# Attention on one Trainium2 core: the six working PSUM banks shared out anew between row maxima and scores

## The reference, cut to what matters

```python
# B, T, C = 8, 1024, 256; 16 heads of 16; fp32
x = x + 0.5 * ffn(layernorm(x))          # 8 experts, top 1, capacity 1024
x = x + attention(layernorm(x))
x = x + 0.5 * ffn(layernorm(x))

def attention(x):
    q, k, v = rope(x @ Wq.T + bq), rope(x @ Wk.T + bk), x @ Wv.T + bv
    att = (q @ k.T) / 4                  # per batch and head, 1024 x 1024
    att = where(causal, att, -1e10)
    att = softmax(att)                   # the row maximum is taken off first
    return (att @ v) @ Wp.T + bp
```

## Time and profile before

| | before |
|---|---|
| runs | 2608.2, 2610.9, 2621.66 us; median 2610.9 us |
| the profiled execution | 2593.98 us |
| span of its trace | 2592.2 us |
| mean granted TensorE clock | 0.913 |
| TensorE matmuls busy | 2175.9 us (84% of the span) |
| VectorE busy | 1695.1 us (65%) |
| ScalarE busy | 1280.3 us (49%) |
| GpSimd busy | 908.2 us (35%) |

### The profile page before, as it was taken

How to read it: one execution, slowest core, us unless ns; L and a number is a source line. 1 busy time by engine, 2 the same in 40 slices (tenths; PEclk the granted TensorE clock), 3 DMA queues, 4 the chain that set the end, 5 groups by cost and what they waited for, 6 DMA issues and landing times. The chain is left out here.

```text
span 2592.2 us, 42982 instructions
## 1 busy us (share of the span) xinstructions
PE 2175.9 (84%) x14628; PEld 1405.6 (54%) x14628; DVE 1695.1 (65%) x5128; ACT 1280.3 (49%) x2578; POOL 908.2 (35%) x1236
## 2 busy tenths in 40 slices
PE   4279999944799998999999999998994774899997
PEld 2169999933344344444434444443333764799997
DVE  7345655435778888788887878777854662565562
ACT  5334444411266656566566656666771333344443
POOL 3624444234233333333333333331001364344442
PEclk8689999967699999999999999999996775999999
DMA  9563222022544353444435344354405424423220
GB/s 367 191 204 115 74 96 99 26 68 87 135 102 106 97 120 95 109 101 107 110 95 119 88 103 101 87 120 94 87 26 165 138 83 164 139 74 103 81 74 22
DMA packets 187419, 283.24 MB, mean 109 GB/s; under 512 B 14888, under 2 KB 150248, under 8 KB 179008
## 3 DMA queue, kind: packets, MB, share of 16 engines
q1 hardware_dynamic: 172864, 247.12, 35.0%
q0 software_dynamic: 14336, 33.38, 3.7%
HBM read 154.02 MB, written 126.88 MB: 108 GB/s over the span
## 5 line engine op out<-in xcount | busy, mean ns | idle before, releaser
L1770 ACT ACTIVATE at_probs<-at_score_ps 128x512 f32<-128x512 f32 (+3 forms) x1536 | 692.2, 497 | 452.9 <-PE at_score_ps L1890 313.4
L1639 DVE CUSTOM_DVE_ANT_0 at_junk<-at_max_ps,at_causal 128x128 f32<-128x128 f32 (+3 forms) x1024 | 485.6, 484 | 127.4 <-PE at_max_ps L1876 125.3
L1876 PE MATMUL at_max_ps<-at_k,at_q 96*128 96x512 bf16 (+3 forms) x1536 | 493.9, 340 | 51.0 <-DVE at_peak L1639 31.2
L1887 PE MATMUL at_score_ps<-at_q,at_k 99*128 99x512 bf16 (+3 forms) x1536 | 499.1, 332 | 13.2 <-DMA at_v<-v_rows 5.4
L1642 DVE TENSOR_REDUCE at_peak<-at_max_ps 128x1 f32<-128x512 f32 x512 | 351.8, 687 | 115.3 <-PE at_max_ps L1876 112.0
L1876 PEld LDWEIGHTS at_max_ps<-at_k,at_q 96*128 96x128 bf16 x1536 | 144.5, 98 | 405.4 <-DVE at_peak L1639 192.4
L1089 DVE TENSOR_TENSOR f_hid_lo<-f_hid,f_hid_hi 128x512 fp32r<-128x512 f32 x256 | 177.5, 693 | 285.4 <-ACT f_hid_hi L1113 285.4
L1110 ACT ACTIVATE f_hid<-f_hid_ps 128x512 f32<-128x512 f32 x256 | 153.1, 598 | 377.9 <-PE f_hid_ps L1136 377.9
L1900 PE MATMUL at_o_ps<-at_probs,at_v 128*32 128x512 f32 (+3 forms) x3072 | 336.2, 510 | 1.3 <-ACT at_probs L1770 0.7
L1151 PE MATMUL f_y_ps<-f_w_hi,f_hid_hi 128*128 128x256 f32 x1024 | 290.9, 284 | 18.5 <-DVE f_hid_lo L1089 18.5
L1151 PE MATMUL f_y_ps<-f_w_hi,f_hid_lo 128*128 128x256 f32 x1024 | 291.2, 284 | 0.0
(11 more groups left out here) (222 smaller groups left out, 3547.4 us busy)
## 6 DMA issues: line engine op xcount, KB each, us to landing
f_w_raw<-in_w SPq DMA_DIRECT2D x32, 1024.0 KB, 7.6
qk<-at_parts SPq DMA_DIRECT2D x32, 768.0 KB, 4.2
expert_in<-r_zeros SPq DMA_DIRECT2D x16, 1040.0 KB, 12.7
f_xe<-expert_in SPq DMA_DIRECT2D x32, 520.0 KB, 6.6
v_rows<-at_v_outs SPq DMA_DIRECT2D x32, 512.0 KB, 6.2
at_v<-v_rows SPq DMA_DIRECT2D x32, 512.0 KB, 10.4
o_rows<-at_o_out SPq DMA_DIRECT2D x64, 256.0 KB, 2.0
at_q<-qk SPq DMA_DIRECT2D x32, 384.0 KB, 7.8
```

Source lines behind the costliest of these rows:

```text
L1639: v.tensor_tensor_reduce(junk[bank(k, r)][:, 0:w], src, causal[:, HALF - w:HALF], 1.0, LEAST, ALU.add, ALU.max, out).then_inc(max_used, 1)
L1770: a.activation(probs[t % 2][:, h, c0:c0 + w], score_ps[(GH * t + h) % BANKS][:, 0:w], ACT.Exp, scale=float(SCALE)).then_inc(exp_done, 1)
L1876: te.matmul(max_ps[bank(u, r)][:, 0:w], q[u][0:ROWS, h, i * P:(i + 1) * P], kk[u][0:ROWS, h, k0:k0 + w], start=True, stop=True).then_inc(m ...
L1887: last = te.matmul(out[:, 0:w], kk[u][:, h, j * P:(j + 1) * P], q[u][:, h, hf * HALF + c0:hf * HALF + c0 + w], start=True, stop=not diagonal)
```

## The change

Two bank counts take the place of one: two banks for scores, four for maxima. The semaphores' starting values and thresholds follow. The masked maxima write their masked values back over their own source in PSUM, and the `junk` tiles are gone. Of the early preparation, the v product goes to the output's bank and the two rotated tiles to the two score banks. The function `bank` takes the group in place of the slot, since the number of places is not a multiple of four.

```diff
--- before.py
+++ after.py
@@ -47,7 +47,7 @@
 ROWS_M = ROWS + PARTS
 VW = 2 * D
 SLOTS = 3
-BANKS = 3
+SCORE_BANKS, MAX_BANKS = 2, 4
 STEPS = [(0, j) for j in (0, 3, 2, 1)] + [(1, j) for j in (0, 7, 6, 5, 4, 1, 2, 3)]
 NS = len(STEPS)
 HALF = S // 2
@@ -1206,7 +1206,6 @@
         causal = sb("causal", [P, HALF], F32)
         hide = sb("hide", [P, P], F32)
         hide_bf = sb("hide_bf", [P, P], BF16)
-        junk = [sb(f"junk{k}", [P, HALF], F32) for k in range(BANKS)]
         stats = sb("stats", [P, 2, 6], F32)
         moments = sb("moments", [P, 2, 2], F32)
         half = sb("half", [P, 2], F32)
@@ -1239,8 +1238,8 @@
         o_out = [sb(f"o_out{k}", [P, HALF], F32) for k in range(2)]
         sums = sb("sums", [P, H * S // P], F32)
 
-        score_ps = [ps(f"score_ps{k}", [P, HALF]) for k in range(BANKS)]
-        max_ps = [ps(f"max_ps{k}", [P, HALF]) for k in range(BANKS)]
+        score_ps = [ps(f"score_ps{k}", [P, HALF]) for k in range(SCORE_BANKS)]
+        max_ps = [ps(f"max_ps{k}", [P, HALF]) for k in range(MAX_BANKS)]
         o_ps = ps("o_ps", [P, HALF])
         prep_ps = ps("prep_ps", [P, 2 * C])
 
@@ -1323,14 +1322,14 @@
 
             return NR * g + (0 if isinstance(g, int) and g == GROUPS else r)
 
-        def bank(k, r):
-
-            return place(k, r) % BANKS
-
-        EARLY_XT, EARLY_QK, EARLY_V, EARLY_ROT = max_ps[0], max_ps[1:3], score_ps[0], score_ps[1:3]
-
-        def peaks_in_ps(k, r):
-            return max_ps[bank(k, r)][:].bitcast(BF16)[0:PARTS * GH, 0:HALF]
+        def bank(g, r):
+
+            return place(g, r) % MAX_BANKS
+
+        EARLY_XT, EARLY_QK, EARLY_V, EARLY_ROT = max_ps[0], max_ps[1:3], o_ps, score_ps
+
+        def peaks_in_ps(g, r):
+            return max_ps[bank(g, r)][:].bitcast(BF16)[0:PARTS * GH, 0:HALF]
 
         @block.sync
         def _(sp):
@@ -1473,7 +1472,7 @@
             def move_peaks(g, u, half):
 
                 at = place(g, RING.index(FIRST)) if half == 0 else place(g + 1, RING.index(SECOND))
-                wait_apart(pool, max_used, at + BANKS + 1, sh.passed)
+                wait_apart(pool, max_used, at + MAX_BANKS + 1, sh.passed)
                 p.dma_start(q[u][ROWS:ROWS_M, :, half * HALF:(half + 1) * HALF], peak_t[:]
                             ).then_inc(peak_loaded[half], 16)
 
@@ -1627,16 +1626,16 @@
                     whose = g if half == 0 else g - 1
                     wait_apart(dve, max_ready, place(g, r) + 1, sh.passed)
                     dve.wait_ge(peak_loaded[1 - half], 16 * (whose + half))
-                    v.tensor_copy(peak_t[:], peaks_in_ps(k, r)).then_inc(max_used, 1)
+                    v.tensor_copy(peak_t[:], peaks_in_ps(g, r)).then_inc(max_used, 1)
                     return
                 half, n = RING[r]
                 h, i, k0, w, diagonal = ITEMS[half][n]
                 i -= half * TPB // 2
                 wait_apart(dve, max_ready, place(g, r) + 1, sh.passed)
                 out = (peak2 if k0 else peak[half])[:, i, h:h + 1]
-                src = max_ps[bank(k, r)][:, 0:w]
+                src = max_ps[bank(g, r)][:, 0:w]
                 if diagonal:
-                    v.tensor_tensor_reduce(junk[bank(k, r)][:, 0:w], src, causal[:, HALF - w:HALF], 1.0, LEAST,
+                    v.tensor_tensor_reduce(src, src, causal[:, HALF - w:HALF], 1.0, LEAST,
                                            ALU.add, ALU.max, out).then_inc(max_used, 1)
                 else:
                     v.tensor_reduce(out, src, AX.X, ALU.max).then_inc(max_used, 1)
@@ -1645,7 +1644,7 @@
 
                 at = (3 + 4) * g + 3 * half
                 if stage == 0:
-                    dve.wait_ge(max_used, (place(g, RING.index((1, 0))) if half == 0 else place(g + 1, 0)) + BANKS)
+                    dve.wait_ge(max_used, (place(g, RING.index((1, 0))) if half == 0 else place(g + 1, 0)) + MAX_BANKS)
                 else:
                     dve.wait_ge(peak_step, at + stage)
                 if half == 1:
@@ -1663,7 +1662,7 @@
                     v.tensor_tensor(peak_part[:, :, 2, :], peak_rest[:], peak_part[:, :, 1, :], ALU.subtract
                                     ).then_inc(peak_ready, 1)
 
-            dve.sem_inc(max_used, BANKS)
+            dve.sem_inc(max_used, MAX_BANKS)
             v.memset(kk[0][ROWS:ROWS_M], 1.0)
             measure(0)
             dve.wait_ge(w_hi_ready, 1)
@@ -1767,10 +1766,10 @@
                 act.wait_ge(pv_done, NS * g + t + 1)
                 for h in range(GH):
                     act.wait_ge(score_ready, GH * (NS * g + t) + h + 1)
-                    a.activation(probs[t % 2][:, h, c0:c0 + w], score_ps[(GH * t + h) % BANKS][:, 0:w],
+                    a.activation(probs[t % 2][:, h, c0:c0 + w], score_ps[(GH * t + h) % SCORE_BANKS][:, 0:w],
                                  ACT.Exp, scale=float(SCALE)).then_inc(exp_done, 1)
 
-            act.sem_inc(exp_done, BANKS)
+            act.sem_inc(exp_done, SCORE_BANKS)
             act.sem_inc(o_copied, 1)
             act.wait_ge(w_loaded, 16 * 3)
             a.copy(w_hi[:], w_raw).then_inc(w_hi_ready, 1)
@@ -1866,14 +1865,14 @@
                     pe.wait_ge(peak_ready, 2 * g + 1 if RING[r] == FIRST else 2 * g)
                     wait_apart(pe, max_used, place(g, r) + 1, sh.passed)
                     for i in range(TPB // 2):
-                        last = te.transpose(peaks_in_ps(u, r)[:, i * P:(i + 1) * P],
+                        last = te.transpose(peaks_in_ps(g, r)[:, i * P:(i + 1) * P],
                                             peak_part[:, i].rearrange("p a h -> p (a h)"), sh.ident_bf[:])
                     last.then_inc(max_ready, 1)
                     return
                 half, n = RING[r]
                 h, i, k0, w, _ = ITEMS[half][n]
                 pe.wait_ge(max_used, place(g, r) + 1)
-                te.matmul(max_ps[bank(u, r)][:, 0:w], q[u][0:ROWS, h, i * P:(i + 1) * P], kk[u][0:ROWS, h, k0:k0 + w],
+                te.matmul(max_ps[bank(g, r)][:, 0:w], q[u][0:ROWS, h, i * P:(i + 1) * P], kk[u][0:ROWS, h, k0:k0 + w],
                           start=True, stop=True).then_inc(max_ready, 1)
 
             def scores(g, u, t, h):
@@ -1883,7 +1882,7 @@
                 if t in FIRST_STEP.values() and h == 0:
                     pe.wait_ge(peak_loaded[hf], 16 * (g + 1))
                 pe.wait_ge(exp_done, GH * (NS * g + t) + h + 1)
-                out = score_ps[(GH * t + h) % BANKS]
+                out = score_ps[(GH * t + h) % SCORE_BANKS]
                 last = te.matmul(out[:, 0:w], kk[u][:, h, j * P:(j + 1) * P],
                                  q[u][:, h, hf * HALF + c0:hf * HALF + c0 + w], start=True, stop=not diagonal)
                 if diagonal:
@@ -1893,7 +1892,7 @@
             def times_v(g, u, t):
                 c0, w, _ = columns(STEPS[t])
                 hf, j = STEPS[t]
-                pe.wait_ge(exp_done, GH * (NS * g + t + 1) + BANKS)
+                pe.wait_ge(exp_done, GH * (NS * g + t + 1) + SCORE_BANKS)
                 if t == FIRST_STEP[hf]:
                     pe.wait_ge(o_copied, 2 * g + hf + 1)
                 for h in range(GH):
```

## The result

The changed kernel takes 2663.9 us (median of 4 runs, 2659.4 to 2665.9), the kernel before 2614.2 in the same comparison (4 runs, 2608.2 to 2621.7): a ratio of 1.0186 with a 95% interval of [1.0154, 1.0219], 49.7 us more. The forecast was 2653 in a range from 2613 to 2689, and slower. The size and the sign hold. Of the terms of its sum, three are right to a few hundredths of a microsecond, three are not.

A forecast was written before the change was run, and what follows sets the result against it. Waits between engines bound the loop, with VectorE the bound first and TensorE later in each prepared group. 26 groups at +1.18 us (+31), the last six +7 and the clock +4 gave +42 on 2610.9: 2653 us, range 2613 to 2689.

The forecast's parts named there:

- The walk through the VectorE stretch: First part of a prepared group, VectorE nearly full: with two score banks, waits for exponentials make TensorE 1.06 us later.
- The TensorE stretch: Later part of a prepared group, TensorE nearly full: score waits add 0.28 us in step 10 and 0.06 in step 8.
- The gain at the start of the next ring: At a group's end, before the next step 0 scores: four maxima banks let head 2 start 0.22 us earlier.
- The last six groups: The six groups behind the 26 with preparation: each was given the same 1.2 us loss, +7 us.
- The clock: Whole loop: more TensorE idling may bring clock falls (+22 us) or the new rhythm avoid them (-22); +4 taken.
- The write into PSUM: Masked maxima writing into PSUM instead of SBUF: bounded at -13 to +13 ns an operation, 0 us taken.
- A: ScalarE's exponentials come earlier, as TensorE starts scores sooner: -0.97 us in each of 31 groups, 2581 us; chance 0.10.
- B: New TensorE waits end under VectorE's backlog from four filled maxima banks: only +4 us left, 2615; chance 0.12.
- C: Reading and writing one bank halves VectorE's rate in the masked maxima: at least +164 us, 2775; chance 0.05.
- signs that I named: New profile: group 41.4 to 41.6 us, step 4 score wait about 2 us, VectorE idle 0.7 us, few maxima waits.

The follow-up runs named there:

- The experiment on the copy: Against the changed kernel: only ScalarE's copy of the second transposed tile moved from behind step 3's to behind step 4's exponentials; 2647.41 us, ratio 1.0126.
- (a): Against the changed kernel: masked values go to bf16 tiles in SBUF, still two score and four maxima banks; 2658.86 us, ratio 1.0177.
- (b): Against the changed kernel: three maxima banks instead of four, two score banks, masked values to fp32 tiles in SBUF; 2663.71 us, ratio 1.0183.

## Why the prediction was right, and where it was not

**The walk through the VectorE stretch, +1.06: right.** Times from the start of the group (1388.61 before, 1436.71 now):

| | before | predicted | measured |
|---|---|---|---|
| scores, step 2 head 2 | 2.97 | 3.60 | 3.60 |
| scores, step 3 head 1 | 4.17 | 5.09 | 5.04 |
| scores, step 4 head 2 | 7.20 | 9.22 | 9.26 |
| maxima matmul behind them | 8.55 | 10.57 | 10.59 |
| VectorE on its result | 10.36 | 11.1 | 11.16 |
| scores, step 6 head 2 | 14.65 | 15.71 | 15.71 |
| TensorE behind the low part of x | 18.09 | 19.15 | 19.16 |

The seven times came out within 0.06 us since each is a sum of durations that were in the trace already; only the order of two engines' queues was needed beside them. The experiment on the copy shows that the cause is the right one as well: without it in the way, step 4's scores come 0.78 us earlier and the group is 41.29 us long.

**The TensorE stretch, +0.28 and +0.06: right.** The timeline of the changed kernel that answers to the earlier trace rows, with VectorE's sum behind its last maxima:

```profile
1467.16 0.10 PEld L1886 LDWEIGHTS at_score_ps<-at_q,at_k 99*128 99x128 bf16 x1 [0.58 <-ACT at_probs L1769]
...
1475.25 0.38 PE L1886 MATMUL at_score_ps<-at_q,at_k 99*128 99x512 bf16 x1
...
1476.13 0.69 DVE L1592 TENSOR_TENSOR at_qk<-at_prep_ps,at_bias 128x512 f32<-128x512 f32 x1
```

The scores that answer to 1417.67 start at 1467.16, that is 29.06 and 30.45 us into the group: +1.39, where 1.06 + 0.28 + 0.06 = 1.40 was written.

**The gain at the start of the next ring, -0.22: this step failed.** The group ends at +1.50 instead of +1.18. The scores of step 0 head 2 did come a little earlier against the rest: 37.27 us before, 38.54 now, +1.27 after +1.39. But the step looked only at TensorE's queue. Beside it runs a second path, VectorE's last maxima, its sum of q and k with the bias (line 1592: 37.95 before, 1476.13 now is 39.42), and GpSimd's product behind that. It has no part in the gain and came +1.47. Where both paths meet, the small VectorE operation lasts until GpSimd's ends: 0.57 us for 0.37, which gives back 0.20. So its end lies 1.88 us (before) and 1.89 (now) behind the start of VectorE's sum, however early its maxima are ready, the transposes of the maxima 0.15 behind that, and the next group's first scores move by the 1.47 of this path. Of these 1.47, 1.42 came with TensorE (the last masked maximum of 512 starts at 36.25 before, 37.67 now) and 0.05 with the masked operations behind it, which last longer when they write into PSUM. Taking GpSimd away from that place brings the group to 41.36 us, 0.44 less, about what the operation lost: 0.57 - 0.17 = 0.40. That the meeting itself stretches the operation is shown by these runs; how the two engines exclude one another is not. The Trainium skill (SBUF — State Buffer, the section on SBUF's two separate sides) says that a VectorE operation with two SBUF inputs and a GpSimd one that reads SBUF share a port pair that one of them holds for its whole instruction. The rows of the section on GpSimd's operation agree in that the one ends with the other; but an operation that began only when GpSimd's was over would end its own 0.17 us behind it, and these end 0.03 us behind.

**The last six groups, +7: mis-sized, they cost 15.9.** I gave each of them the 1.2 us of a prepared group. A group without preparation costs 34.00 - 31.75 = 2.25 us and the last one 26.70 - 22.10 = 4.60. The first of the six, with a remainder of preparation, has the rest, 2.3. The cause is the score bank and not the write or the fourth bank: the variants with two score banks and `junk` tiles take 33.96 and 34.32 us for the same group. What the sum missed is that more heads wait here. The waits of the weight loads before the scores go from 1.4 us (4 waits) to 8.1 (19) in such a group, 6.7 more, and 2.25 comes out; in a prepared group they grow by some 4.5 (39.1 and 122.8 us in 19.5 and 19.0 groups), and 1.5 comes out: a third in both. In the last group, where VectorE has nothing to do, they go from 11.8 to 17.8, and 4.60 comes out. Which of the waits make up these was not followed. The range had taken in three times this term, and 2.3 times it came.

**The clock, +4: wrong in sign.** 26 groups at full clock would take 26 x 40.30 = 1047.8 us before and 26 x 41.80 = 1086.8 now. The windows say 1064.4 and 1095.7, so the falls and all other deviations cost 16.6 us before and 8.9 now: -8. It is the falls that changed: of the 24 groups from 733 to 1716 us nine had a mean clock of 0.96 and took 13.2 us beyond full-clock groups, and of the 24 that answer to them (763 to 1773) three now do, for 5.0. The mean granted clock of the loop went from 0.98 to 0.99. Each is one execution, but the variants agree: eight such groups with the write alone and ten with the copy moved, both with three and three banks, none with (a), four with (b). The number of banks isn't the rule either: with GpSimd's operation moved three and three banks have three, and two and four banks have eight groups below 1.00 with the copy and VectorE's use of it moved. The argument that more idle time of TensorE brings more falls does not hold from before to after; with four and two banks TensorE waits still more, and its clock is 0.96. So what the clock will do is not to be read from the sum of the waits, and I have no better rule.

**The write into PSUM, 0: right for the kernel's time, not quite for a group.** The two rows bounded an operation at -13 to +13 ns; it is +8 to +18 by form, with 58 ns more in the accumulator's read, which no row had priced. A group at full clock pays some 0.05 us for it: 40.30 and 40.36 with three and three banks, 41.72 and 41.77 with two and four. The experiment with that part alone gives 1.0001 [0.9989, 1.0012]. The estimate from the figure of the Trainium skill (VectorE: DVE Perf Modes, the section on the TRN2 errata), +65 ns an operation and +22 us for the kernel, is refuted for the operation itself. The section gives its figures by the place of the source; to carry them over to the target was my step. The read of the accumulator grew by 58 ns, beside other work.

**The sum.** 26 x 1.50 = 39.0, minus 7.7 for the clock and what else deviates, plus 15.9 is 47.2; forecast were 31 + 4 + 7 = 42. The errors of +8, -12 and +9 us partly cancel: that the total came near is owed to this luck as well as to the walk.

**The rivals.** A (faster) and B (no difference) rest on the fourth bank being worth something or the score waits lying hidden. The pair with three and four maxima banks beside two score banks refutes both: 1.0183 and 1.0177. C (a masked operation at half its rate) fell with 497 ns in place of 484. Four of the signs that I named were off. The group is 41.8 us, not 41.4 to 41.6. The longest wait before the scores is 1.35 us in step 4, not about 2: the walk moved the start by 2.02, but some 0.9 of that is TensorE's own lateness from the steps before, which is no wait. VectorE stands 0.55 us before the first maxima of 512, not 0.7. And the waits of line 1875 for line 1638 did not go: 149 of 182 us stayed, which fits with their lying where VectorE is the bound.

## What to carry to other kernels

A buffer is worth what the wait it removes is worth on the engine that bounds that stretch: 183.8 us of waits for the maxima were bait, since the fourth bank only moved them to the next wait, while the small total before the scores (72 us) was held down by the very bank that was given away. Before you take a buffer from a ring, list what else stands in the consumer's queue (here one copy of 0.58 us ahead of four exponentials): with one buffer less, moving this item brought 0.51 us a group back, and with the third buffer it brought nothing. And follow all the paths that meet at the end of a stretch, GpSimd's too, before you book a gain there.

## What the hardware showed that was not expected

- A small VectorE operation with two inputs in SBUF (128x16) takes 0.17 us alone and up to 0.58 beside a GpSimd operation, and ends with it. A `tensor_scalar` of 128x256 fp32 has a mean of 538 to 581 ns in the one arrangement, where a GpSimd operation lies beside the first half of the pair, and 909 to 948 in the other, where GpSimd works beside nearly all of it. Moving GpSimd away from one of them moved it onto the other: 12.3 us gained with two and four banks, nothing with three and three.
- A masked maximum that writes its fp32 result into the bank from which it reads takes 8 to 18 ns more than one that writes to SBUF, and the read of its accumulator 140 ns instead of 82. A group pays some 0.05 us for both, which the kernel's time does not show.
- More waiting on TensorE came with fewer groups below the full clock (nine of 24 to three), and still more of it with more (21 of 24 with four and two banks). Moving one GpSimd operation, with three and three banks, took them from nine to three as well. Why the rhythm matters is open.
